# Cross-attention and sparse feed-forward on one core: the second normalisation and the gate factors in one block, and a second buffer for half of the turned probabilities

## The reference

```python
n = layernorm(x)
q = n @ Wq                                  # 32 heads of 128
k, v = concat(ctx, n) @ Wk, concat(ctx, n) @ Wv   # 4 groups of 128, 461 keys a batch
o = softmax(q @ k.T / sqrt(128)) @ v
x = x + o @ Wo
m = layernorm(x)
inter = m @ c1_w.T @ c2_w.T                 # rank 16, then 3584
idx = argmax(inter.reshape(tokens, 56, 64)) + 64 * arange(56)
h = relu(einsum('bkm,bm->bk', w1[idx], m))
out = x + einsum('bk,bkm->bm', h, w2t[idx])
```

## Time and profile before

| what | value |
|---|---|
| median of 3 runs | 3652.81 us (3650.86 to 3655.02) |
| time of the profiled execution | 3654.5 us |
| its span | 3652.8 us |
| attention, first score to last output product | about 1188 to 2005 us |
| project_out | 2006 to 2605 us |
| second normalisation | 2610.75 to 2643.7 us |
| gate factors | 2644.0 to 2668.6 us |
| hidden layer | from 2668.86 us |
| busy share of PE, DVE, ACT, POOL | 94%, 63%, 37%, 24% |

### The profile page before, as it was taken

The page is one execution under the profiler, slowest core; times in us unless marked ns, Lnnn a source line. Parts: engine busy times, 40 slices in busy tenths (PEclk is TensorE's granted clock), DMA queues, the critical chain, the costliest instruction groups (busy, mean ns, idle before and its releaser), DMA issues. The chain is left out here.

```text
span 3652.8 us, 51935 instructions
## 1 busy us (share of the span) xinstructions
PE 3448.0 (94%) x18370; PEld 3060.2 (84%) x18370; DVE 2295.6 (63%) x3858; ACT 1369.2 (37%) x2560; POOL 881.1 (24%) x1100
## 2 busy tenths in 40 slices
PE   6999999799999999999999899999789999989999
PEld 5888888799999888888888688688589999977877
DVE  5555576777765677777776433433368888766775
ACT  3333344343432776777776322322411111121120
POOL 0000000000000766676665100000001111135443
PEclk8999999899999999999999899999889999999999
DMA  3333332454443333333332644644313444488886
GB/s 125 95 101 107 101 96 79 117 139 120 118 123 106 111 109 106 107 95 102 106 107 60 198 123 120 187 119 120 115 68 132 150 151 147 147 304 313 263 289 215
DMA packets 477859, 501.44 MB, mean 137 GB/s; under 512 B 172548, under 2 KB 372228, under 8 KB 477652
## 3 DMA queue, kind: packets, MB, share of 16 engines
q1 hardware_dynamic: 441988, 371.79, 34.3%
q0 software_dynamic: 34608, 124.90, 10.1%
q10 hardware_dynamic: 1056, 2.10, 0.2%
HBM read 383.68 MB, written 115.02 MB: 137 GB/s over the span
## 5 line engine op out<-in xcount | busy, mean ns | idle before, releaser
L2083 PE MATMUL wo_acc<-wo_w,wo_l 128*128 128x512 f32 (+1 forms) x2496 | 576.0, 393 | 23.3 <-DVE wo_l L2033 23.3
L427 PE MATMUL kv_bank<-kv_wo,kv_so 128*128 128x512 f32 x2436 | 574.1, 395 | 16.4 <-DVE kv_wo L519 11.0
L2083 PEld LDWEIGHTS wo_acc<-wo_w,wo_l 128*128 128x128 f32 (+1 forms) x2496 | 462.5, 186 | 136.6 <-DVE wo_w L2057 25.3
L427 PEld LDWEIGHTS kv_bank<-kv_wo,kv_so 128*128 128x128 f32 x2436 | 457.6, 190 | 110.9 <-issue 17.4
L815 PE MATMUL pr_bank<-pr_xo,pr_wp 128*128 128x400 f32 x2688 | 498.8, 347 | 28.9 <-ACT pr_s L882 13.4
L815 PEld LDWEIGHTS pr_bank<-pr_xo,pr_wp 128*128 128x128 f32 x2688 | 493.6, 190 | 31.7 <-DVE pr_wp L899 24.0
L26 PE MATMUL hid_acc<-x1t,hid_w 128*128 128x336 f32 x2688 | 442.6, 323 | 1.4 <-DVE c_raw L1827 0.9
L2352 PE MATMUL w_acc<-w_w,w_l 128*128 128x512 f32 (+1 forms) x1848 | 422.0, 391 | 12.1 <-DVE w_l L2291 12.1
L26 PEld LDWEIGHTS hid_acc<-x1t,hid_w 128*128 128x128 f32 x2688 | 426.4, 194 | 2.1 <-issue 1.1
L2352 PEld LDWEIGHTS w_acc<-w_w,w_l 128*128 128x128 f32 (+1 forms) x1848 | 339.5, 184 | 94.4 <-DVE w_l L2291 12.3
L1311 PE MATMUL outs<-pt,v 128*128 128x384 f32 (+3 forms) x1536 | 347.1, 348 | 28.6 <-issue 14.4
(11 more groups left out here) (185 smaller groups left out, 4034.8 us busy)
## 6 DMA issues: line engine op xcount, KB each, us to landing
wo_l_raw<-o_scratch SPq DMA_DIRECT2D x192, 256.0 KB, 2.9
pair_raw<-in_L_xattn_Wq_dram SPq DMA_DIRECT2D x64, 512.0 KB, 5.8
q_scratch<-pr_out SPq DMA_DIRECT2D x128, 200.0 KB, 2.4
o_scratch<-o_stage SPq DMA_DIRECT2D x64, 400.0 KB, 3.6
q_raw<-q_scratch SPq DMA_DIRECT2D x64, 384.0 KB, 3.1
stage<-in_ctx_dram SPq DMA_DIRECT2D x45, 512.0 KB, 3.9
h_scratch<-c_raw SPq DMA_DIRECT2D x28, 672.0 KB, 5.5
wo_w_raw<-in_L_xattn_Wo_dram SPq DMA_DIRECT2D x16, 1024.0 KB, 7.0
```

The source lines that it names most:

```text
L427: last = pe.matmul(bank[:, BANK[i], :], so[:, i, a, c, :], wo[:, i, e, c, :], start=(not opened and c == 0 and (a, e) == PAIRS[0]), stop=( ...
L2083: last = pe.matmul(acc[p][:rows, :], l[j % 2][:, a, k, :rows], w[:, c, m * per + k, :], start=(m == 0 and k == 0 and (a, c) == PAIRS[0]), ...
```

## The change

In `attend`, `pt` is split: `pt_first` (tiles 0 to 2) stays single, `pt_second` (tiles 3 to 5 and the tail's columns) has two buffers, one for groups of even and one of odd number. `bring_tail(G)` waits for the h = 1 product of group G-2 instead of G-1, and is called two steps earlier.

`normalise` and `gate_weights` are gone; `second_norm_and_gates` does both in one block. Nine gate banks (two of c1, seven of c2) are transposed first, through two PSUM banks instead of eight. Then the 13 tiles follow, with three PSUM buffers instead of four; ScalarE scales even tiles, GpSimd odd ones. The products for `zs` are made in four groups of tiles (512, 384, 384 and 320 columns), the first three in between the tiles, the last behind them. c1 and c2 are written four times instead of three (0, 32, 64, 96), and c1's low part goes into columns 96 to 111 of the same array as the high part, so that a group takes two matmuls for each chunk instead of three. The first two blocks of w1 are loaded in this block, behind the tiles.

```diff
-        pt = sb("pt", [P, 2, NC, cols], F32R)
+        pt_first = sb("pt_first", [P, 2, NC, split], F32R)
+        pt_second = [sb(f"pt_second{i}", [P, 2, NC, cols - split], F32R) for i in range(2)]
...
-                if G:
-                    pool.wait_ge(o_full, 2 * G)
-                pool.tensor_copy(pt[:, :, :, body:], pt_tail[:, :, :, g * left:(g + 1) * left]).then_inc(tail_in, 1)
+                if G >= 2:
+
+                    pool.wait_ge(o_full, 2 * (G - 1))
+                pool.tensor_copy(pt_second[G % 2][:, :, :, body - split:],
+                                 pt_tail[:, :, :, g * left:(g + 1) * left]).then_inc(tail_in, 1)
...
-                if j >= 0 and place(j)[2] == 3:
+                if j >= 0 and place(j)[2] == 1:
                     bring_tail(place(j)[1])
...
-GATE_STARTS = (0, 32, 64)
+GATE_STARTS = (0, 32, 64, 96)
...
+    rounds = 2 + blocks // per
+    R, B, GB = 8, 3, 2
+    zg = [(0, 4), (4, 7), (7, 10), (10, NT)]
...
+            for p in range(2):
+                sp.dma_start(w1_raw[p][:, :], w1[p * P:(p + 1) * P, :]).then_inc(w1_landed[p], 16)
...
+            pool.wait_ge(step, 8)
+            for t in by_pool:
+                n = tiles[t][1]
+                pool.wait_ge(x_in[t % R], 16 * (t // R + 1))
+                pool.tensor_scalar(raw[t][:n, :], raw[t][:n, :], small[:n, 5, t:t + 1], small[:n, 6, t:t + 1],
+                                   ALU.mult, ALU.add).then_inc(ready_pool, 1)
...
+            for r in range(rounds):
+                high_gate(r)
+            act.wait_ge(step, 8)
+            scale(0)
+            scale(2)
+            for t in range(NT):
+                high_part(t)
+                if t % 2 == 0 and t + 4 < NT:
+                    scale(t + 4)
+                for g in range(NZ):
+                    if t == min(zg[g][1] + 1, NT - 1) and g < NZ - 1:
+                        high_gate(rounds + g)
+            high_gate(rounds + NZ - 1)
...
+            def gate_bank(r):
+                if r >= GB:
+
+                    pe.wait_ge(g_done, r - GB + 1)
...
+            def factors(g):
+                lo, hi = columns(g)
+                gate_bank(rounds + g)
+                pe.wait_ge(low, zg[g][1])
+                for c in range(chunks):
+                    for b in range(2):
+                        last = pe.matmul(banks[:, (rounds + g) % GB, :hi - lo], c1t[:, c, :], x1t[:, b, c, lo:hi],
+                                         start=(c == 0 and b == 0), stop=(c == chunks - 1 and b == 1))
+                last.then_inc(g_full, 1)
...
+            for t in range(NT):
+                turn(t)
+                for g in range(NZ):
+                    if t == min(zg[g][1] + 1, NT - 1) and g < NZ - 1:
+                        factors(g)
+            factors(NZ - 1)
...
-            load(0, 0)
-            load(1, 1)
```

More of the change, by code:

```diff
@@ L42, in _ @@
             pool.tensor_copy(ident_bf[:, :], ident[:, :]).then_inc(made, 1)
[L45 to L175, removed]
-                    act.wait_ge(landed[t % R], 16 * (t // R + 1))
-                    act.activation(raw[t][:n, :], raw[t][:n, :], ACT.Identity,
-                                   scale=small[:n, 5, t:t + 1], bias=small[:n, 6, t:t + 1]).then_inc(ready, 1)
-                    if not own and t >= 2:
-                        high_part(t - 2)
-                if own:
-                    high_part(first)
-                    if g + 1 < len(groups):
-                        root(g + 1, *groups[g + 1])
-                    for t in range(first + 1, end):
-                        high_part(t)
-            if not own:
-                high_part(NT - 2)
-                high_part(NT - 1)
-        @block.tensor
[L192 to L197, removed]
-                for c in range(chunks):
-                    last = pe.transpose(turned_ps[t % B][:, c, :n], raw[t][:n, c * P:(c + 1) * P],
-                                        ident[:n, :n])
-                last.then_inc(turned, 1)
@@ L1468, in _ @@
             for r in range(rounds):
-                if 2 + r >= 8:
-                    pe.wait_ge(done, r - 5)
+                gate_bank(r)
                 for k in range(per):
-                    last = pe.transpose(banks[:, (2 + r) % 8, k * P:(k + 1) * P], c2_raw[:, per * r + k, :], ident[:, :])
-                last.then_inc(full, 1)
-            for t in range(4):
-                pe.wait_ge(done, 2 + t)
-                product(pe, banks[:, 1 + t, :width], lambda a, c: c1t[:, a, c, :],
-                        lambda a, c: x1t[:, a, c, t * width:(t + 1) * width], chunks).then_inc(full, 1)
@@ L1495, in _ @@
[L1495 to L1512 removed]
+                    at = banks[:, r % GB, k * P:(k + 1) * P]
@@ new lines, in _ @@
+                    if r < 2:
+                        last = pe.transpose(at, c1_raw[:, (4 * r + k) * P:(4 * r + k + 1) * P], ident[:, :])
+                    else:
+                        last = pe.transpose(at, c2_raw[:, per * (r - 2) + k, :], ident[:, :])
+                last.then_inc(g_full, 1)
+            for t in range(NT):
+                turn(t)
+                for g in range(NZ):
+                    if t == min(zg[g][1] + 1, NT - 1) and g < NZ - 1:
+                        factors(g)
@@ L1574, in hidden_layer @@
     parts = ((sparse.S, 8), (sparse.S + 8, tt - 8 - sparse.S))
-    landed, turned = [sem(f"w1_landed{i}") for i in range(2)], sem("w1_turned")
+    turned = sem("w1_turned")
     high, low = sem("w1_high"), sem("w1_low")
@@ L1587, in sb @@
             return mem.enter_context(nc.sbuf_tensor("hid_" + n, shape, dt))
-        raw = [spare[0], sb("raw1", [P, hidden])]
         w = [sb(f"w{i}", [P, 2, chunks, P], F32R) for i in range(2)]
@@ L1600, in hidden_layer @@
         base = keys[:, :sparse.groups]
-        ring = [sb(f"ring{i}", [P, hidden]) for i in range(slots)]
+        ring = [spare[0]] + [sb(f"ring{i}", [P, hidden]) for i in range(1, slots)]
         gate = mem.enter_context(nc.psum_tensor("gate", [P, 2, 512], F32))
```

180 lines of the change are left out of this document (128 added, 52 removed).

## The result

The changed kernel takes 3596.96 us (median of 4 runs, 3591.09 to 3598.34), against 3652.7 us on the same chip (3650.86 to 3655.02): a ratio of 0.9844, 95% interval 0.9827 to 0.9861. That is 55.7 us less; 59.7 us less was predicted. The profiled execution took 3598.34 us, its span is 3596.6 us, so 56.2 us less than the span before.

| stage | before | after | difference | predicted |
|---|---|---|---|---|
| start to attention's first score | 1188.0 | 1188.6 | +0.6 | 0 |
| attention, first score to last copy | 816.8 | 774.7 | -42.1 | -42 |
| `project_out`, first transfer to the start of its last addition | 597.9 | 600.7 | +2.8 | +0.5 |
| from there to the merged block's first transfer | 6.65 | 6.01 | -0.6 | 0 |
| normalisation and gates, to the start of the hidden layer's queues | 58.1 | 47.7 | -10.4 | -13 |

What follows compares the result with a forecast made beforehand. The prediction took TensorE, busy 94% of the span, as the bound, except between `project_out` and the hidden layer. Its terms, -42 - 13 - 5 + 0.5 = -59.5 us, gave a forecast of 3593 us, range 3580 to 3615.

Steps and rivals of the forecast that it cites:

- Attention, -42 us: In attention, casting the tail's columns two steps earlier on GpSimd ends 61 TensorE stops, gaining 42 us; bounds 0 and 49.
- The correction of 0.12 us: In attention, each stop costs TensorE's queue 0.11 or 0.12 us less than its recorded idle: 49.3 us recorded becomes 42.0.
- The merged block, -13 us: Normalisation and gates in one block take 45 us instead of 58.1, gaining 13 us; bounds 2 and 15.
- I add 2 us for c1, some c2 banks and the first tiles at the lower level: Merged block's allowance for TensorE starting at clock 0.50: 2 us on top of 42.8 us at full clock.
- The round of 2.05 us: Merged block: one gate buffer's cycle of transposes, ScalarE, VectorE and handing over, 2.05 us, about 1.03 us a bank.
- My sign against the prediction: Merged block: a clock staying at 0.50 beyond 10 us would show the prediction wrong.
- GpSimd's scaling, 1.46 us: Merged block: GpSimd scales each second tile in 1.46 us, bounds 1.23 us and twice 1.46, without reaching TensorE.
- The hidden layer's start, -5 us: Hidden layer: w1 already loaded gains 3.6 us, higher clock and no gate wait 1.4 us; 3.5 us if clock is low.
- The fourth load, +0.5 us, 0 to 2: In `project_out`, one more load of c1 and c2 meets other transfers and costs 0.5 us, bounds 0 to 2.
- A, another wait in attention: Rival: another wait takes over in attention and gives back half, 21 us, for 3614 us; chance 0.12.
- B: Rival: merged block gives little, transposes at lower clock until the first product group, 7 us less, 3600 us; chance 0.11.
- C, less clock in attention: Rival: TensorE without its stops gets less clock in attention, making the kernel slower, about 3680 us at 0.90; chance 0.02.

Runs made afterwards that it cites:

- w1 late: The changed kernel with the first two blocks of w1 loaded at the start of the hidden layer, as before the change; 3601.03 us, ratio to before 0.9864.

## Why the prediction was right, step by step

- **Attention, -42 us: right, -42.1.** Both kinds of wait were the tail's cast, shown by the kernel in which the cast alone moves back. The correction of 0.12 us for each of 61 stops was needed: the recorded 49.3 us would have been 7 us too many. The lead, 3 to 4 us by the prediction, is 2.1 to 4.9 us. At its shortest GpSimd has a 1.30 us piece of the next batch's `v` in its queue ahead of the cast's new place (1902.05), which I had not counted. Which half of the edit does the work, the prediction left open; it is the place in the queue.
- **The merged block, -13 us: -10.4, mis-sized.** The step that failed is "I add 2 us for c1, some c2 banks and the first tiles at the lower level". At full clock the block is 43.2 us (42.8 predicted); the half clock lasted 19.5 us and cost 4.5 us: 1.8 us until the tiles start (13.8 against 12.0 us) and 2.7 us behind that (33.9 against 31.2 us). There the first two tiles take 3.67 - 1.97 = 1.7 us more, and the last product group 3.92 - 2.58 = 1.3 us. The round of 2.05 us was right at full clock (2.06) and 2.52 us here. My sign against the prediction, a clock of 0.50 beyond 10 us, thus came; its price was 2.5 us. The size of the term hangs on the execution: in the three profiles with a block of 45.4 to 45.5 us the half clock cost 2.2 us, close to the 2 us that I added.
- **GpSimd's scaling, 1.46 us: 1.20 us,** just under the lower bound of 1.23 us, and hidden, as predicted. Without it the block takes 2.6 us more at a like clock.
- **The hidden layer's start, -5 us: -5.7,** shown by w1 late (5.6 us).
- **The fourth load, +0.5 us, 0 to 2: about 2.5, outside its bounds.** I sized it by TensorE's loss in 2084 to 2090 us, where the third copies land, and not by the tiles that come late while they do. The load of c2 is 3584 rows of 64 bytes, and its cost probably goes with the rows, which no run here separates from the bytes. In the earlier trace rows the DMA engines are as full with 156 GB/s there as with 392 GB/s in the normalisation. The Trainium skill ("DMA: Bandwidth & Descriptors", Why small descriptors are slow) gives each packet a fixed overhead besides its bytes; the two rates agree with that.
- **Rivals.** A, another wait in attention: it did not come; the spare time at VectorE's low part stayed at 0.67 us. B: the longer half clock came, but ended some 4 us before the first product group, so 2.5 us of its 7. C, less clock in attention: excluded by attention's 774.7 us.

The sum was -59.5 us and the profiled execution shows -56.2 us: the two misses, 2.6 and 2.3 us, less 0.7 us at the hidden start and 0.9 us of drift in stages that the change does not touch. What stays open is why `project_out` differs between executions (600.7 and 597.6 us in the two profiles of the changed kernel, 6.2 us among all eight with four loads), and why the merged block's clock comes up early in some executions and not in others; the first is at least as large as the fourth load's price, which therefore rests on the waits for `wo_l` more than on the stage's length.

## What to carry to other kernels

Where a short instruction on a helping engine gates the bottleneck, look first at its place in that engine's queue: moving one call gave 42 us without any buffer. Where TensorE starts from idle, give it its work in one piece, even at the price of waits later: two-buffer rounds with gaps of 0.55 us and more kept the clock at 0.50 for 7 to 19.5 us, an unbroken row of transposes for 4.8 to 5.7 us (in two of three profiles it fell back once more, which cost 1.0 us). Before two versions of such a block are compared by their lengths, look at the clock in both: 48.0 against 47.8 us hid 2.6 us here. And size an added transfer by the tiles that it makes late, and look at its rows as well as at its bytes.

## What the runs showed of the hardware

The clock stayed at 0.50 with TensorE busy for 6.78 of 9.00 us, and rose to 1.00 by 3.6 us once the first gaps held transposes; it then stayed there with TensorE busy for 3.77 of 6.00 us. Transposes alone were enough for that. With the same work of TensorE in the same place its mean over the first 18.6 us was 0.50 in two executions and 0.63 to 0.65 in four. GpSimd scaled 128 x 1024 fp32 elements in 1.20 us, ScalarE in 1.23 us.
